# Expert layers whose rows move block by block through per-expert DRAM regions, in place of a sort, a gather and a scatter in each layer

## The chip, the cores and the metric

The kernel runs on one core of a Trainium2 chip. The metric is the device time of one execution in microseconds (us), as the median of several runs. Within the core work TensorE (PE: matrix products and transposes), VectorE (DVE), ScalarE (ACT) and GpSimd (POOL); SyncE (SP) and POOL issue the transfers between DRAM and the on-chip memory. Each engine takes its instructions in the order of the program and waits at semaphores for the others.

## The reference

2,048 tokens (32 sequences of 64) of 128 numbers go through three stages, each added to the running value x after a layer norm: a cross attention with 16 heads over 128 context rows, a linear recurrence over time, and four routed expert layers that share the weights of 16 experts (W1 is 128 x 512 and W2 512 x 128 for each, in float32). All of this document happens in the last stage:

```
def _unipool_layer(xt, router, W1, W2):       # xt is 2048 x 128, router 128 x 16
    probs = softmax(xt @ router);  w = max(probs);  idx = argmax(probs)
    for each expert i:  acc += where(idx == i, w, 0) * (silu(xt @ W1[i]) @ W2[i])
    return acc
xt = layernorm(x)
for router in routers: xt = _unipool_layer(xt, router, W1, W2)     # 4 layers, no residual between
x = x + xt
```

A layer's input is the output of the layer before it, so the routing of a layer can only begin when outputs of the layer before are there.

## The kernel before

Attention runs over 16 tiles of 128 tokens, the recurrence over all tokens at once; neither is touched but for where x and its normalised copy are held. Then come the four layers, as a loop of two passes over two layers (`layers`). Each layer has two stages.

**Routing** works on all 16 tiles at once. SP loads the 2,048 rows (four transfers, L253), PE transposes them (L696), ACT and DVE copy the transposes out, PE makes the logits (L734) and turns them (L739). A chain of some 40 DVE instructions (L1042 to L1117) takes the softmax, counts for each token how many tokens of its expert stand before it, with the help of products on PE (L750 to L755), and so finds the token's place in an order sorted by expert; two further DVE and POOL steps and 16 products (L763) invert that order. From it come a list `token_i` of the sorted tokens and the tables `piece_expert` and `piece_tile`. PE fills its waits with products that nobody reads (`stay_warm`, L689).

**Pieces.** The sorted rows are 16 tiles; where an expert ends inside a tile the tile is worked on twice, so a layer has up to 31 pieces (`PIECES`), and all 31 are always run. POOL gathers the rows of a tile by an indirect transfer (L382), PE transposes it (L782), ACT copies the transpose out (L525) and copies the W1 of the piece's expert to a fixed buffer (L522); PE makes the hidden units (L793, 4 products, each float32 product in two passes), ACT takes the tanh of half of them (L531), DVE makes silu from that (L1132), PE multiplies with W2 (L806, again 4 products), and DVE adds the result, times the routing weight, to `ysort` (L1142). Each step of the loop `step(i)` holds the turn of tile i, the hidden units of piece i-1 and the output of piece i-2. When a sorted tile is complete, POOL writes its rows back to their tokens' places in DRAM by an indirect transfer (L389). The next layer's load waits for all of these. After the last layer the rows are loaded once more, added to x and stored (L1151, L262).

The lines are printed here as far as the change touches them.

Of the kernel before, what the change touches and what calls it, by code (L numbers as in the profile page):

```python
# [22 lines left out]
def perceiver_block(nc, x, ctx, mask, Wq, bq, Wk, bk, Wv, bv, Wo, bo, A, Wb, bb, Wc, bc, Wd, bd,  # L23
# [15 lines left out]
    PIECES = NT + E - 1  # L39
    PC = 32  # L40
    FC = FF // P
    FIRST = 4
    PAIRS = HEADS // 2
    NV = 5
    assert D == P and T == P and S * 2 == P and NG == 4 and E == 16 and L % 2 == 0

    x_t = x.rearrange("b s d -> (b s) d").rearrange("(t p) d -> p t d", p=P)
    out_t = out.rearrange("b s d -> (b s) d").rearrange("(t p) d -> p t d", p=P)
    ctx_t = ctx.rearrange("b t d -> t b d")
    rows = [nc.dram_tensor(f"token_rows_{i}", (N, D), F32, kind="Internal").ap() for i in range(2)]  # L50
# [4 lines left out]
    with ExitStack() as stack:  # L55
# [3 lines left out]
        def sem(name):  # L59
# [11 lines left out]
        rnow = sb("rnow", [P, 32])  # L71
# [17 lines left out]
        iota_r = sb("iota_r", [P, P])  # L89
        iota_j = sb("iota_j", [P, PC])  # L90
        iota_e1 = sb("iota_e1", [1, E])
        sorted_pos = sb("sorted_pos", [P, NT])
        not_first = sb("not_first", [P, GW])
        not_first16 = sb("not_first16", [P, 256])
        vals = sb("vals", [P, NT, NV], BF16)

        xs = sb("xs", [P, NT, D])
        cur = sb("cur", [P, NT, D])
# [24 lines left out]
        lgT = sb("lgT", [P, 512])  # L123
        ex, eq, nth, rk = (sb(n, [P, 256]) for n in ("ex", "eq", "nth", "rk"))
        ohb = sb("ohb", [P, 256], BF16)
        mx, sm, wt, ends, starts, place, wr = (sb(n, [P, 16]) for n in
                                               ("mx", "sm", "wt", "ends", "starts", "place", "wr"))
        place_i, row_i, tile_i = (sb(n, [P, NT], I32) for n in ("place_i", "row_i", "tile_i"))
        ohr = sb("ohr", [P, NT, P], BF16)
        oht = sb("oht", [P, NT, NT], BF16)  # L130
        carried = sb("carried", [P, NT, NV, NT], BF16)
        token_i = sb("token_i", [P, NT], I32)
        token, expert_at, piece_at, wsort = (sb(n, [P, NT]) for n in ("token", "expert_at", "piece_at", "wsort"))
        ends_cmp = sb("ends_cmp", [P, NT, E])
        piece_hot = sb("piece_hot", [P, PC, NT])
        wpiece = sb("wpiece", [P, PC])
        end_i = sb("end_i", [1, E], I32)
        first_piece = sb("first_piece", [1, E])
        pcmp = sb("pcmp", [1, PC, E - 1])
        pexp, pexp_tile = sb("pexp", [1, PC]), sb("pexp_tile", [1, PC])  # L140
        piece_expert = sb("piece_expert", [1, PC], I32)
        piece_tile = sb("piece_tile", [1, PC], I32)


        xin = ppT[:, 2, :].rearrange("p (u d) -> p u d", u=4)
        xT = vm[:].rearrange("p u n x -> p (u n x)")[:, 0:N]
        ysort = sb("ysort", [P, NT, D])
        th, hh, w1_piece = pp[:, 0:2, :], pp[:, 2:4, :], ppT[:, 0:2, :]

        names = """x_first_loaded x_loaded w_loaded later_loaded w1_loaded w2_loaded stored rows_stored  # L150
            consts_pool consts_dve consts_mm dve_step act_step
# [4 lines left out]
            router_ready logits_done lgT_ready lg_done sh_ready ex_ready oh_ready rank_mm  # L156
            tiles_hot carried_ready inv_in inv_done tokens_ready pieces_ready y_zeroed
            nmax_ready xo_ready rden_ready rstd_ready
            waited_alone xT_mm xT_evac w1_staged h_mm tanh_done h_ready y_mm y_ready
            out_ready""".split()  # L160
        s = dict(zip(names, [sem(n) for n in names]))
        ctx_loaded = [sem(f"ctx_loaded{u}") for u in range(2)]
# [30 lines left out]
        def piece_steps(step):  # L193


            for i in range(PIECES + 2):
                step(i)
# [980 lines left out]
```

## Time and profile before

| what | value |
|---|---|
| median of 3 runs | 573.17 us (569.8, 573.17, 573.19) |
| span of the profiled execution | 577.5 us, 4.3 us over the median |
| up to the first transpose of layer 1 | 188.3 us |
| routing of layer 1, up to the first transpose of a gathered tile | 24.8 us |
| pieces of the four layers | 63.96, 63.86, 64.02, 65.84 us |
| between the layers | 30.22, 32.87, 30.50 us |
| after the last product | 13.17 us |
| busy over the span | PE 85%, PE weight loads 69%, DVE 57%, ACT 48%, POOL 34% |

The profiled execution has no device time of its own beside its span, so the span stands for it. A stage is best read by its own borders: the first transpose of a gathered tile (L782) opens the pieces of a layer, the last output product (L806) closes them. PE's busy share in the routing stages is mostly `stay_warm`, so it says nothing on what bounds those.

### The profile page before, as it was taken

What the parts mean: (1) busy time and instruction counts of PE and PEld (TensorE: products, weight loads), DVE (VectorE), ACT (ScalarE), POOL (GpSimd) and SP (SyncE); (2) the same over time, 40 slices, a digit from 0 to 9 for tenths busy, and PEclk for the clock granted to TensorE, in tenths of its full rate; (3) what the DMA queues carried; (4) which work ended last, traced back from release to release, by engine and by line L of the source; (5) the groups of instructions that cost most, each with busy time, mean ns of one, the idle gap of its engine ahead of it and who ended that gap; (6) DMA issues with size and microseconds to landing.
All of it is one profiled execution on the core that took longest, in us unless ns stands there. A gap on an engine that the chain in (4) does not pass through costs nothing.

```text
span 577.5 us, 16903 instructions
## 1 busy us (share of the span) xinstructions
PE 490.8 (85%) x5788; PEld 400.5 (69%) x5788; DVE 330.0 (57%) x746; ACT 276.8 (48%) x684; POOL 196.7 (34%) x243
## 2 busy tenths in 40 slices
PE   1589999999787769999868999976899986799894
PEld 1367877787554338999435999733899953589892
DVE  2468777877658684455185455339345526645452
ACT  1277766777672316665103666410566610266550
POOL 8222332231030154235325405503532541541352
PEclk9999999999999889999997999978899999799998
DMA  5542223300000201001301100120110130100005
GB/s 142 178 130 85 66 86 94 93 5 4 3 1 2 73 18 35 24 20 40 91 1 37 33 8 37 41 74 5 42 31 10 39 100 3 32 28 16 24 37 159
DMA packets 37315, 28.12 MB, mean 49 GB/s; under 512 B 5105, under 2 KB 33137, under 8 KB 37233
## 3 DMA queue, kind: packets, MB, share of 16 engines
q1 hardware_dynamic: 33136, 18.62, 11.2%
q0 software_dynamic: 4096, 8.40, 4.6%
q8 instruction: 52, 0.85, 0.6%
q14 instruction: 31, 0.25, 0.1%
HBM read 20.71 MB, written 6.29 MB: 47 GB/s over the span
## 4 chain that ended last, share of the span: by engine, by line
PE 59%; DVE 15%; issue 7%; DMA 6%; ACT 5%; POOL 3%; another core or an unknown queue 2%; SPq 1%; DVEq 0%; POOLq 0%; ACTq 0%
PE bank L806 18%; PE bank L793 18%; PE bank L635 6%; PE bank L616 4%; DMA cur<-token_rows 3%; PE bank L594 3%; DVE ohr L1083 2%; DVE ppT L910 2%; DMA ppT<-token_rows,token_i 2%; DMA token_rows<-ysort,token_i 2%; PE bank L588 1%; PE bank L575 1%; PE bank L564 1%; PE bank L782 1%
## 5 line engine op out<-in xcount | busy, mean ns | idle before, releaser
L1132 DVE SCALAR_TENSOR_TENSOR pp<-pp,bank 128x512 f32<-128x512 f32 x124 | 85.3, 688 | 126.8 <-ACT pp L531 116.0
L806 PE MATMUL bank<-w,pp 128*128 x992 | 136.3, 281 | 9.0 <-DVE pp L1132 6.9
L793 PE MATMUL bank<-vm,ppT 128*128 x992 | 137.4, 283 | 0.0
L806 PEld LDWEIGHTS bank<-w,pp 128*128 128x128 f32 x992 | 122.5, 194 | 11.7 <-issue 10.9
L793 PEld LDWEIGHTS bank<-vm,ppT 128*128 128x128 f32 x992 | 125.1, 198 | 1.6 <-issue 0.5
L531 ACT ACTIVATE pp<-bank 128x512 f32<-128x512 f32 x124 | 74.1, 598 | 95.6 <-PE bank L793 77.8
L522 ACT COPY ppT<-w 128x512 f32 x124 | 75.8, 611 | 60.2 <-DVE piece_tile L1105 59.7
L389 POOL DMA_INDIRECT token_rows<-ysort,token_i x64 | 62.1, 971 | 102.9 <-DVE ysort L1142 85.2
L382 POOL DMA_INDIRECT ppT<-token_rows,token_i x64 | 61.7, 964 | 64.2 <-PE bank L782 41.3
L689 PE MATMUL bank<-trib,onesb 128*128 128x512 bf16 x308 | 77.4, 409 | 0.0
L446 ACT ACTIVATE pp<-bank,nmax 128x128 f32<-128x128 f32 x256 | 68.0, 426 | 0.0
L689 PEld LDWEIGHTS bank<-trib,onesb 128*128 128x128 bf16 x308 | 31.6, 105 | 37.3 <-issue 9.3
L318 POOL TENSOR_TENSOR qm<-qT,own_head 128x256 f32<-128x256 f32 x32 | 19.0, 614 | 85.0 <-ACT kT L436 85.0
L895 DVE TENSOR_REDUCE nmax<-bank 128x4 f32<-128x512 f32 x64 | 41.0, 684 | 11.4 <-PE bank L594 11.4
L1142 DVE SCALAR_TENSOR_TENSOR ysort<-bank,wpiece,ysort 128x128 f32 x124 | 42.9, 346 | 7.5 <-PE bank L806 6.1
L616 PE MATMUL bank<-ident,pp 128*128 128x128 f32 x256 | 40.8, 282 | 7.3 <-DVE ppT L910 5.7
L616 PEld LDWEIGHTS bank<-ident,pp 128*128 128x128 f32 x256 | 27.4, 141 | 14.7 <-ACT pp L446 10.1
L454 ACT COPY ppT<-bank 128x512 f32<-128x512 f32 x32 | 18.9, 590 | 32.8 <-PE bank L616 32.8
L373 POOL TENSOR_TENSOR carried<-oht,vals 128x256 bf16<-128x256 bf16 x12 | 12.4, 1057 | 56.4 <-DVE oht L1074 56.4
L910 DVE COPY ppT<-bank 128x512 f32<-128x512 f32 x32 | 20.7, 686 | 9.1 <-PE bank L635 8.8
L782 PE MATMUL bank<-ident,ppT 128*128 128x128 f32 x64 | 18.3, 285 | 6.3 <-DMA ppT<-token_rows,token_i 6.3
L594 PEld LDWEIGHTS bank<-kT,qm 32*128 32x128 f32 x512 | 16.5, 194 | 7.2 <-issue 7.2
(182 smaller groups left out, 522.8 us busy)
## 6 DMA issues: line engine op xcount, KB each, us to landing
w<-in_L_ffn_W_dram SPq DMA_DIRECT2D x32, 256.0 KB, 3.4
cur<-token_rows SPq DMA_DIRECT2D x16, 256.0 KB, 3.6
cx<-in_ctx_dram SPq DMA_DIRECT2D x16, 128.0 KB, 2.4
token_rows<-cur SPq DMA_DIRECT2D x1, 1024.0 KB, 5.0
ppT<-token_rows,token_i POOLq DMA_INDIRECT x64
token_rows<-ysort,token_i POOLq DMA_INDIRECT x64
out_dram<-xs SPq DMA_DIRECT2D x4, 256.0 KB, 2.7
xs<-in_x_dram SPq DMA_DIRECT2D x1, 768.0 KB, 6.1
```

The source lines that it names most:

```text
L382: g.indirect_dma_start(out=xin[:, i % 4, :], out_offset=None, in_=src, in_offset=bass.IndirectOffsetOnAxis(ap=token_i[:, i:i + 1], axis=0)) \
L389: g.indirect_dma_start(out=dst, out_offset=bass.IndirectOffsetOnAxis(ap=token_i[:, i:i + 1], axis=0), in_=ysort[:, i, :], in_offset=None). ...
L446: last = a.activation(pp[:, r, k * T:(k + 1) * T], banks[r][:, k * T:(k + 1) * T], ACT.Exp, bias=nmax[:, r, k:k + 1], scale=1.0)
L522: a.copy(w1_piece[:, i % 2, :], w1[:, ds(e * FF, FF)]).then_inc(s["w1_staged"], 1)
L531: a.activation(th[:, j % 2, :], banks[2 + j % 2][:, :], ACT.Tanh, scale=0.5) \
L616: last = nc.tensor.transpose(bank[:, k * P:(k + 1) * P], pp[:, r, k * P:(k + 1) * P], ident[:])
L689: mm(bank[:, :].rearrange("p (k t) -> p k t", k=4), onesb[:], trib[:].unsqueeze(1).broadcast_to([P, 4, P]), start=True, stop=True)
L793: last = mm(banks[2 + j % 2][:, c * P:(c + 1) * P], w1_piece[:, j % 2, c * P:(c + 1) * P], xT[:, ds(tile_of[j] * P, P)], start=True, stop= ...
L806: last = mm(banks[6 + j % 2][:, 0:D], hh[:, j % 2, c * P:(c + 1) * P], w2[:, ds(e * FF + c * P, P)], start=(c == 0), stop=(c == FC - 1))
L895: v.tensor_reduce(out=nmax[:, r, :], in_=banks[r][:, :].rearrange("p (k t) -> p k t", k=4), axis=AX, op=ALU.max, negate=True).then_inc(s[" ...
L1132: v.scalar_tensor_tensor(hh[:, j % 2, :], th[:, j % 2, :], 1.0, banks[2 + j % 2][:, :], ALU.add, ALU.mult).then_inc(s["h_ready"], 1)
L1142: v.scalar_tensor_tensor(sorted_tile, banks[6 + j % 2][:, 0:D], wpiece[:, j:j + 1], sorted_tile, ALU.mult, ALU.add).then_inc(s["y_ready"], 1)
```

## The change

The sort, the gather and the second indirect transfer go. A token's row travels as 274 numbers (1,096 bytes): its value, its 16 logits for the coming layer, a stamp, its token number, and x (`ROW`). There are two DRAM buffers with a region of 2,176 rows for each expert and one spare. In each layer up to 31 blocks of 128 rows are loaded from the regions by plain transfers (`load_rows`, SP, one for each block, at a row number read from `block_row`), computed, and the new rows are scattered by expert into the other buffer (`scatter_part`, POOL). The logits of the next layer are made block by block: PE turns each block's output (`turn_output`) and multiplies it with the next router (`next_logits`). DVE picks the expert of a part of 1 to 4 blocks (`choose`), PE ranks (`ranks`), DVE gives places (`put`), POOL scatters the part. After the last part DVE makes the tables of the next layer (`make_tables`). The routing weight is worked out beside the blocks, for four groups of blocks (`gate_shift`, `gate_finish`), from the logits in the loaded rows. ACT takes silu in one instruction. The last layer adds x and scatters straight to the output, 31 indirect transfers. The loop over layers is written out. The rows for the pads of all regions are written once, during attention, by two SP transfers of 128 x 17 x 274 numbers. W1 stays on chip in both versions and ACT copies it block by block into one of two buffers.

```diff
-            def one_layer(layer, parity, two):      # POOL: 16 gathers, then 16 scatters
-                for i in range(NT):                 # L382
-                    g.indirect_dma_start(out=xin[:, i % 4, :], out_offset=None, in_=src, ...)
-                for i in range(NT):                 # L389
-                    wait_alone(pool, s["y_ready"], layer * PIECES + (i + E))
-                    g.indirect_dma_start(out=dst, ..., in_=ysort[:, i, :], in_offset=None)
+            def scatter_part(number, of_part, region):                          # POOL
+                wait_alone(pool, s["place_ready"], number + 1)
+                for j in of_part:
+                    g.indirect_dma_start(
+                        out=region, out_offset=bass.IndirectOffsetOnAxis(ap=place_i[:, j:j + 1], axis=0),
+                        in_=slots[:, j, :], in_offset=None, bounds_check=E * REGION - 1, oob_is_err=False) \
+                        .then_inc(s["scattered"], 16)
-            def load_next(layer, source): ...       # SP: four loads of 256 KB, L253
+            for layer in range(L):                                              # SP
+                sp.wait_ge(s["scattered"], 16 * (NT + layer * BLOCKS))
+                sp.wait_ge(s["tables_ready"], 2 * layer + 2)
+                for j in range(BLOCKS):
+                    load_rows(layer, j)
+        parts = [list(range(a, min(a + 4, 24))) for a in range(0, 24, 4)] + [[24, 25, 26], [27, 28, 29], [30]]
+        gate_groups = [(0, 4), (4, 10), (10, 20), (20, BLOCKS)]
+        gate_steps = [0, 4, 9, 16]
+                for i in range(BLOCKS + 4):                                     # ACT
+                    if i < BLOCKS:
+                        stage_w1(layer, i)
+                    if 0 <= i - 1 < BLOCKS:
+                        silu(layer, i - 1)
+                    if 0 <= i - 3 < BLOCKS and layer < L - 1:
+                        evac_yT(layer, i - 3)
+                    if i in gate_steps:
+                        gate_half_tanh(layer, gate_steps.index(i))
+            stay_warm(banks[7], 50)                                             # PE, ahead of layer 1
+            def turn_output(layer, j):
+                pe.wait_ge(s["y_evac"], n + 1)
+                nc.tensor.transpose(banks[4][:, 0:P], tile_n(j), ident[:]).then_inc(s["yT_mm"], 1)
+            def next_logits(layer, j):
+                pe.wait_ge(s["yT_evac"], n + 1)
+                mm(banks[7][:, 0:E], yTs[:, n % 2, :], rt[:, layer + 1, :], start=True, stop=True)
+                for i in range(BLOCKS + 4):                                     # PE
+                    ... turn(i), hidden(i - 1), turn_output(i - 3), next_logits(i - 4), output(i - 2)
+                        for m, of_part in enumerate(parts):
+                            if of_part[-1] == (i - 4 if i == BLOCKS + 3 and m == len(parts) - 1 else i - 5):
+                                ranks(part_number(layer, m), len(of_part))
+                if layer < L - 1:
+                    stay_warm(banks[7], 30)
+            def gate_shift(layer, k):                                           # DVE
+                lo, hi = gate_groups[k]
+                for j in range(lo, hi):
+                    dve.wait_ge(loaded[j], 16 * (layer + 1))
+                for i in range(BLOCKS + 6):                                     # DVE
+                    ... evac_xT(i), gate_shift at 0, 4, 9, 16, gate_finish one step later,
+                    ... evac_logits(i - 4), evac_y(i - 2), put of the part that ends at i - 5,
+                    ... choose of the part that ends at i - 4
+                if layer < L - 1:
+                    make_tables()
```

PE, one step of the block loop in a layer (`pp` holds the hidden units, `ppT` and `slots` the rows, `w_piece` the copied W1). Before, for a step with a gathered tile:

```order
L782 MATMUL bank<-ident,ppT 128x128
L793 ISA
L793 MATMUL bank<-vm,ppT 128x128 x2
L200 TENSOR_LOAD piece_tile
L793 MATMUL bank<-vm,ppT 128x128 x2
L200 TENSOR_LOAD piece_expert
L806 ISA
L806 MATMUL bank<-w,pp 128x128
```

The L806 pair stands four times there. With the change, a step after which a part of four blocks is ranked:

```order
L202 TENSOR_LOAD block_expert
L775 MATMUL bank<-ident,slots 128x128
L784 MATMUL bank<-xTs,w_piece 128x128 x4
L803 MATMUL bank<-ident,slots 128x128
L810 MATMUL bank<-rt,yTs 128x16
L794 ISA
L794 MATMUL bank<-w,pp 128x128
...
L753 MATMUL bank<-ohb,onesb 128x64
L757 MATMUL bank<-ohb,trib 128x48
L753 MATMUL bank<-ohb,onesb 128x48
L753 MATMUL bank<-ohb,onesb 128x32
L753 MATMUL bank<-ohb,onesb 128x16
L758 MATMUL bank<-ohb,trib 128x16
```

All 31 blocks now have a turn, and a second one, a product of 16 columns and a share of the ranking are new; the 8 large products are the same.

DVE, the end of a layer with the change, from the places of the part of blocks 27 to 29 on (before, some 40 rows of routing stood between two layers):

```order
L1054 TENSOR_TENSOR rk<-bank,next_at 128x48
L1056 TENSOR_TENSOR rk<-rk,ohb 128x48
L1057 TENSOR_REDUCE place<-rk 128x3
L1061 TENSOR_TENSOR place_i<-outside,place 128x3
L1063 TENSOR_TENSOR next_at<-next_at,bank 128x16
L1044 TENSOR_REDUCE mx<-slots 128x1
...
L1061 TENSOR_TENSOR place_i<-outside,place 128x1
L1063 TENSOR_TENSOR next_at<-next_at,bank 128x16
L1070 TENSOR_TENSOR blocks_i<-next_at,round_up 128x16
...
L1078 TENSOR_SCALAR block_row<-first_row,lane_rows 128x1
L1080 TENSOR_SCALAR block_expert<-expert 128x1
```

The last two rows end `make_tables`, on which SP's first load and ACT's and PE's first block wait.

SP between two layers. Before:

```order
L207 ISA
L207 REGISTER_ALU
L253 DMA cur<-token_rows 128x4x128 x4
L257 REGISTER_ALU
L257 COMPARE_AND_BRANCH
```

With the change, the pads' two transfers and the first loads (with what they wait for):

```order
L244 DMA expert_rows<-slots 128x17x274 x2
L202 TENSOR_LOAD block_row [waits tables_ready,scattered,pads_written]
L250 ISA
L250 DMA slots<-expert_rows 128x274
L202 TENSOR_LOAD block_row
```

Four loads became 31, each with a table entry read into a register ahead of it.

## Rows read from the trace of the kernel before

**Rows 1.** Busy time by stage; columns: stretch, length, busy us (count) of PE, PEld, DVE, ACT, POOL, clock, DMA.

```profile
188.26:213.06 24.80, 17.01 (x98) 8.49 (x99) 18.71 (x51) 5.50 (x11) 7.21 (x7) 0.86 0.16 45
213.06:277.02 63.96, 61.07 (x513) 59.91 (x514) 30.94 (x64) 37.23 (x77) 27.00 (x29) 0.97 0.10 32
277.02:307.24 30.22, 21.96 (x127) 10.13 (x125) 17.97 (x48) 2.21 (x4) 8.79 (x8) 0.94 0.14 42
307.24:371.10 63.86, 61.10 (x513) 59.85 (x514) 30.82 (x64) 37.28 (x77) 27.05 (x29) 0.97 0.10 32
371.10:403.97 32.87, 24.34 (x127) 11.04 (x124) 18.07 (x48) 3.49 (x5) 8.87 (x9) 0.84 0.13 40
403.97:467.99 64.02, 61.17 (x513) 59.95 (x514) 30.93 (x64) 37.25 (x77) 26.96 (x29) 0.97 0.10 32
467.99:498.49 30.50, 21.98 (x127) 10.14 (x125) 18.04 (x48) 2.21 (x4) 8.85 (x9) 0.94 0.14 42
498.49:564.33 65.84, 61.73 (x513) 60.03 (x514) 31.08 (x64) 37.27 (x77) 26.98 (x29) 0.97 0.10 30
564.33:577.50 13.17, 6.04 (x29) 2.55 (x26) 3.12 (x5) 0.00 (x0) 3.50 (x3) 0.83 0.59 169
```

**Rows 2.** Timeline, weight loads; columns: start, duration, instruction, count: pieces without turns.

```profile
247.99 0.97 PEld L793 LDWEIGHTS bank<-vm,ppT 128*128 128x128 f32 x8
260.50 0.97 PEld L793 LDWEIGHTS bank<-vm,ppT 128*128 128x128 f32 x8
```

**Rows 3.** Timeline, weight loads of the turns: twelve pieces with a turn, first and last.

```profile
222.57 0.14 PEld L782 LDWEIGHTS bank<-ident,ppT 128*128 128x128 f32 x1
244.24 0.14 PEld L782 LDWEIGHTS bank<-ident,ppT 128*128 128x128 f32 x1
```

**Rows 4.** Timeline, PE: the ranking products in layer 2.

```profile
293.96 1.01 PEld L750 LDWEIGHTS bank<-ohb,onesb 128*128 128x128 bf16 x15
```

**Rows 5.** Timeline: between layers 1 and 2 (an idle time and its releaser stand in brackets).

```profile
275.87 1.15 PE L806 MATMUL bank<-w,pp 128*128 x8 [0.60 <-DVE pp L1132]
277.18 0.35 DVE L1142 SCALAR_TENSOR_TENSOR ysort<-bank,wpiece,ysort 128x128 f32 x1 [1.19 <-PE bank L806]
278.32 0.97 POOL L389 DMA_INDIRECT token_rows<-ysort,token_i  x1 [0.57 <-issue]
280.64 2.01 SPq L253 DMA_DIRECT2D cur<-token_rows  x4
...
303.46 0.17 DVE L1093 TENSOR_TENSOR token_i<-bank,token 128x16 int32<-128x16 f32 x1
304.45 1.23 POOL L382 DMA_INDIRECT ppT<-token_rows,token_i  x1 [3.10 <-DVE token_i L1093]
305.99 0.96 POOL L382 DMA_INDIRECT ppT<-token_rows,token_i  x1 [0.30 <-issue]
307.24 0.33 PE L782 MATMUL bank<-ident,ppT 128*128 128x128 f32 x1 [0.53 <-DMA ppT<-token_rows,token_i]
307.61 0.27 ACT L525 COPY vm<-bank 128x128 f32<-128x128 f32 x1 [0.52 <-PE bank L782]
```

**Rows 6.** Timeline, DVE: two chained instructions of 16 and of 256 numbers.

```profile
295.58 0.17 DVE L1066 TENSOR_TENSOR starts<-ends,bank 128x16 f32<-128x16 f32 x1
295.78 0.42 DVE L1068 TENSOR_TENSOR rk<-bank,starts 128x256 f32<-128x256 f32 x1
```

**Rows 7.** Timeline: ACT's second activation of layer 2, with its idle time.

```profile
314.47 0.60 ACT L531 ACTIVATE pp<-bank 128x512 f32<-128x512 f32 x1 [3.13 <-remote]
```

**Rows 8.** Timeline, DVE: the last transposes copied out in layer 1.

```profile
191.15 0.69 DVE L1032 COPY curT<-bank 128x512 f32<-128x512 f32 x1 [0.85 <-PE bank L696]
```

**Rows 9.** The page's DMA issues: line, engine, count, KB each, median us to landing.

```profile
cx<-in_ctx_dram SPq DMA_DIRECT2D x16, 128.0 KB, 2.4
token_rows<-cur SPq DMA_DIRECT2D x1, 1024.0 KB, 5.0
```

**Rows 10.** Chain of waits: a table entry read into a register (start, us, queue, line).

```profile
275.62 0.30 DVEq L200
```

More of the change, by code:

```diff
@@ new lines, in perceiver_block @@
+        eq, nth, rk, away = (sb(n, [P, 4 * E]) for n in ("eq", "nth", "rk", "away"))
+        ohb = sb("ohb", [P, 2, 4 * E], BF16)
+        place = sb("place", [P, 4])
+        place_i = sb("place_i", [P, BLOCKS], I32)
+        token_i = sb("token_i", [P, BLOCKS], I32)
+        next_at = sb("next_at", [P, E])
+        blocks_i = sb("blocks_i", [P, E], I32)
+        blocks = sb("blocks", [P, E], I32)
+        ends, past, row_at = (sb(n, [P, E]) for n in ("ends", "past", "row_at"))
+        expert, first_row = sb("expert", [P, 1]), sb("first_row", [P, 1])
@@ L536, in _, with stage_w1 @@
-            layers(act, one_layer)
+            for q in (0, 2):
+                act.wait_ge(s["t_done"], 4 + q + 1)
+                a.copy(curT[:, q * 512:(q + 1) * 512], banks[q][:, :]).then_inc(s["t_evac"], 1)
+            a.preload_act_table(ACT.Silu)
+            def stage_w1(layer, j):
+                n = layer * BLOCKS + j
+                e = entry(block_expert, j, mybir.EngineType.Activation, E - 1)
+                if n >= 2:
+                    act.wait_ge(s["h_mm"], n - 1)
+                a.copy(w1_piece[:, n % 2, :], w1[:, ds(e * FF, FF)]).then_inc(s["w1_staged"], 1)
@@ new lines, in silu, with evac_yT @@
+            def silu(layer, j):
+                n = layer * BLOCKS + j
+                act.wait_ge(s["h_mm"], n + 1)
+                if n >= 2:
+                    act.wait_ge(s["y_mm"], n - 1)
+                a.activation(hh[:, n % 2, :], banks[2 + n % 2][:, :], ACT.Silu).then_inc(s["h_ready"], 1)
+            def evac_yT(layer, j):
+                n = layer * BLOCKS + j
+                act.wait_ge(s["yT_mm"], n + 1)
+                if n >= 2:
+                    act.wait_ge(s["lg_mm"], n - 1)
+                a.copy(yTs[:, n % 2, :], banks[4][:, 0:P]).then_inc(s["yT_evac"], 1)
@@ new lines, in _, with turn @@
+            first_logits(0)
+            first_logits(1)
+            ranks(0, 4)
+            first_logits(2)
+            ranks(1, 4)
+            first_logits(3)
+            ranks(2, 4)
+            ranks(3, 4)
+            stay_warm(banks[7], 50)
+            def turn(layer, j):
+                n = layer * BLOCKS + j
+                pe.wait_ge(loaded[j], 16 * (layer + 1))
+                if n >= 2:
+                    pe.wait_ge(s["xT_evac"], n - 1)
+                nc.tensor.transpose(banks[n % 2][:, 0:P], tile_n(j), ident[:]).then_inc(s["xT_mm"], 1)
@@ new lines, in hidden @@
+            def hidden(layer, j):
+                n = layer * BLOCKS + j
+                pe.wait_ge(s["xT_evac"], n + 1)
+                pe.wait_ge(s["w1_staged"], n + 1)
+                if n >= 2:
+                    pe.wait_ge(s["h_ready"], n - 1)
+                for c in range(FC):
+                    last = mm(banks[2 + n % 2][:, c * P:(c + 1) * P], w1_piece[:, n % 2, c * P:(c + 1) * P],
+                              xTs[:, n % 2, :], start=True, stop=True)
+                last.then_inc(s["h_mm"], 1)
```

599 lines of the change are left out of this document (267 added, 332 removed).

## The prediction

> **What bounds the kernel now.** I read the busy time by stage first, because the change leaves everything up to 188 us alone but for where rows are held. The four stretches of pieces take 63.96, 63.86, 64.02 and 65.84 us, with weight loads busy for 60 of 64 us: there PE is the bound. The three stretches between them take 30.22, 32.87 and 30.50 us, together 93.6; PE's products there are filler, and DVE (18 us of 30) and transfers set the pace. The first routing takes 24.8, the end 13.17 [rows 1]. Then the timeline: a piece without a turn repeats every 1.79 us (247.99 to 260.50, seven periods), so one of its 16 passes costs 0.11 [rows 2]; with a turn it is 1.97 (222.57 to 244.24, eleven periods) [rows 3]. Fifteen pieces of 1.79 and sixteen of 1.97 make 58.4; what is left of 63.95, 5.6 us, is the filling of the pipeline. 3.1 of it is one idle time of ACT with a releaser the profile doesn't know [rows 7].
>
> So the change trades: PE gets more to do in each block, where it is the bound, and most of the routing leaves the path between layers.
>
> **The change part by part.** The sum is made against the span of 577.5 us, which is 4.3 over the median; the difference is carried over to the median.
>
> *Up to 188 us: nothing.* POOL's constants change by a few small fills, either way. The pads are two writes of 2.38 MB, issued behind the last weights, when the transfers are nearly idle. At the rate of the 1 MB store (5.0 us) [rows 9] they take some 24 us, and the first scatter is 80 us away. Were that cover gone, SP's first load would wait 24 us.
>
> *Block.* The 8 large products stay: 1.79. Each block has a turn at 0.18, as now [rows 2, 3]; the second turn is one pass between two others, 0.11; the logits two passes whose 16 columns hide no weight load, 0.22; six ranking products for four blocks at 1.01/15 [rows 4], 0.10. That is 2.40. Below, with both turns packed at 0.11, 2.33; above, both at 0.18, 2.47. ACT has the same copy and activation, and a copy of 0.27 [rows 5]: 1.4 of 2.40, covered. DVE has two copies of 0.35, a small one of 0.17, and nine chained instructions of 64 numbers for four blocks. The price of those: 16 numbers take 0.17 and 256 take 0.42, the next starts 0.03 later [rows 6], so 64 take 0.22, with the hop 0.25. With the gates some 1.8 us of 2.40: covered on the mean. The tight place is the second turn: DVE starts on an output 0.16 after the product's end and takes 0.35 [rows 5], while PE has a turn and four hidden products (1.0) ahead of it.
>
> *Filling.* DVE's own silu step (0.69) goes, but DVE now stands at block 0's gates until four rows' loads have landed, and behind it wait the copy of block 1's transpose and ACT's tanh. Loads are spaced by a register read of 0.30 [rows 10] and an issue of 2.01/4 = 0.50 [rows 5], so three more take 2.4. Part of that runs beside ACT's idle time. I take 5.6 - 0.7 + 1.6 = 6.5; bounds 3.4 (no idle time of 3.1) and 8.
>
> *Layers 1 to 3.* 31 x 2.40 + 6.5 = 80.9 for 63.95: 3 x 17.0 = **+50.9**.
>
> *Between layers*, counted from the end of the last output product. Output copied by 0.51; turned by 0.9 (0.33); copied by ACT by 1.2; logits of block 30 by 1.65. Meanwhile the logits of block 29 are copied (1.3), and the part 27 to 29 is chosen, four instructions, by 2.4; ranked by 3.0; its places are there after four more, at 3.95. POOL's first scatter follows its token list by 0.82 (303.63 to 304.45), the next come 1.26 apart [rows 5]. The three of this part and, after a wait of 0.28, that of block 30 bring the last scatter's start to 8.85; block 30's places (6.3) and the tables (8.4) are earlier. From the last scatter's start to SP's load is 2.32 (278.32 to 280.64) [rows 5], the register read 0.30, the landing of 128 KB 2.4 [rows 9]: 13.9. For 93.6 in three now 41.7: **-51.9**. The filler of 30 products ends before that.
>
> *First layer.* The last transposes are copied out at 191.84 [rows 8]; ACT's table load now follows its copies. Logits of the first quarter 0.9 and 0.16, copies and choosing of two quarters 1.3 each, places 1.0: 196.5. POOL starts at 197.3 and issues 16 scatters: 15 x 1.26 and three waits of 0.28 make 217.0 for the last. Then 2.32, 0.30 and 2.4: 222.1 for the first turn, which is at 213.06 now: **+9.0**. All scatters must land ahead of any load; before, tiles came one by one while PE worked. For the filler of 50 products nobody waits.
>
> *Layer 4* has no second turn and no logits: 31 x 1.97 + 6.5 = 67.6 for 65.84: **+1.8**. *End:* last output copied 0.51, POOL 0.82, landing 2.32: 3.65 for 13.17, **-9.5**.
>
> Sum: 50.9 - 51.9 + 9.0 + 1.8 - 9.5 = +0.3. From the median 573.17 that gives **573.5**. What is late next in a layer is again PE.
>
> **A rule weighed.** The 31 loads are spaced 0.80 by SP, and the 1 MB store moves 140 KB in 0.7 [rows 9], so I let SP set the pace. The Trainium skill speaks against the change here: "DMA: Bandwidth & Descriptors", Bandwidth, Measured, gives 0.95 us for 64 KB and 6.15 for 1 MB and calls small transfers descriptor-dominated. Between its two figures 140 KB would take 1.35 us, an estimate, and the sum would be some 22 us more by the count of rival B. The trace has no load of 140 KB.
>
> **The rivals.**
>
> A, *faster: the idle time of filling doesn't come back.* ACT's 3.13 us [rows 7] stand about the third piece of each layer, with no named cause; nothing says that a program without loop has them. Against: two of the four layers don't follow a jump back and have them too. 4 x 3.1 less: 561.
>
> B, *slower: the loads come late.* DVE asks for blocks 4 to 9 at step 4, some 8.2 us after the first turn (filling, then 2.4 a step); at 0.80 the ninth lands at 7.2. It decides from a spacing of 0.91. At half as much again, 1.2, it lands at 10.8: 2.6 late in four layers, 584. For it: register read and address stand in SP's queue ahead of each load; 0.30 is DVE's price, not SP's. Against: the 1 MB store's rate.
>
> C, *slower: POOL's price goes with bytes.* Its 0.97 us are for rows of 512 bytes; at 1,096 they would be 2.08. Exposed are 16 scatters ahead of layer 1 and 4 in each of three gaps: 28 x 1.11 = 31, 604. It decides from 0.2 more for each. Against: gather and scatter of the same 128 rows take 0.96 and 0.97 though one reads and one writes DRAM [rows 5], which fits a price by rows. The same page (SWDGE vs HWDGE vs iDMA) has a GpSimd core compute one pair of descriptors for each operation, by which C falls; no run here shows a longer row.
>
> D, *slower: DVE's order holds PE.* 1.8 us of work in 2.40, in order, with waits for rank products, gates and loads between the copies that PE needs. The gates' six instructions of up to 176 numbers (0.35 each) stand ahead of an output's copy, which then comes 0.3 late. It decides from 0.06 for each block; at 0.15, 93 x 0.15 = 14, 587.
>
> **The numbers.** Forecast 0.33, alone 564 to 582 (block 2.33 to 2.47: 6.5 either way; filling +6). A 0.28, B 0.14, C 0.12, D 0.13. About 1%, 5.7 us, is what a measurement of this kernel tells from no change: 567.4 to 578.9. Of the forecast 0.05 lies below and 0.06 above, of A 0.25 below; of B 0.12, of C 0.11 and of D 0.11 above. So faster 0.30, slower 0.40, within 0.30. The range is 555 (A with the packed block, 561 - 6.5) to 598 (B and D together, 10 + 14, or C at four fifths); it leaves out the rest of C and what lies beyond these mixtures, less than 0.2.
>
> **What would show it.** First turn of layer 1 at 222 (at 240, C). Period of the turns 2.40 in layers 1 to 3 and 1.97 in layer 4; over 2.5 with PE idle on a DVE copy is D. From a layer's last output product to the next layer's first turn 14 us, with POOL's last four scatters 1.26 apart. Idle time of DVE on loads at step 4 is B; no idle of 3 us in ACT's first three activations is A. The prediction is wrong if the block isn't PE's to bound, or if between layers something other than POOL's queue comes last.

## The result, and the profile after

The changed kernel takes **580.15 us** (median of 5 runs, 577.12 to 582.67) against 573.17 (median of 5): 1.0155 times as long, 95% interval 1.0100 to 1.0209. A second comparison gave 578.93 against 570.06, 1.0156 [1.0112, 1.0201]. So the change makes the kernel 1.6% **slower**. In the runs of the changed kernel the time is 1.8 us above the span of the same execution.

The first view to read is the busy time by stage of the changed kernel's profiled execution (span 575.3); it answers to [rows 1] and has their columns: stretch, its length, busy us (count) of PE, PE's weight loads, DVE, ACT, POOL, then granted clock, DMA share, GB/s. The stages are: up to the last transposes, first routing, then a layer and a gap (the stretch from a layer's last output product to the next layer's first turn) in turn, and the end.

```profile
0.00:193.59 193.59, 160.10 (x3237) 122.75 (x3237) 131.26 (x295) 114.37 (x353) 50.66 (x100) 0.97 0.32 91
193.59:227.63 34.04, 21.28 (x123) 12.51 (x122) 12.09 (x57) 4.89 (x10) 15.79 (x16) 0.81 0.21 72
227.63:306.60 78.97, 74.56 (x656) 72.91 (x656) 43.44 (x185) 40.49 (x95) 23.41 (x24) 0.95 0.29 83
306.60:320.59 13.99, 10.58 (x44) 4.62 (x44) 5.50 (x32) 0.88 (x2) 6.81 (x7) 0.76 0.11 25
320.59:398.61 78.02, 73.31 (x657) 71.83 (x655) 43.49 (x185) 40.63 (x95) 23.42 (x25) 0.98 0.28 82
398.61:411.53 12.92, 9.13 (x43) 4.11 (x43) 5.50 (x32) 0.88 (x2) 6.79 (x7) 0.87 0.08 16
411.53:490.94 79.41, 73.41 (x656) 72.01 (x656) 43.50 (x185) 40.72 (x95) 23.41 (x24) 0.98 0.29 83
490.94:504.92 13.98, 10.57 (x44) 4.61 (x43) 5.50 (x32) 0.88 (x2) 6.81 (x7) 0.76 0.13 29
504.92:570.22 65.30, 60.78 (x528) 59.25 (x526) 27.53 (x97) 34.64 (x65) 28.68 (x30) 1.00 0.29 79
570.22:575.29 5.07, 0.00 (x0) 0.00 (x0) 0.35 (x1) 0.00 (x0) 1.41 (x2) 0.79 0.01 0
```

The trade is there as forecast: the gaps fall from 30 to 34 us to 13 or 14, the layers grow to 78 or 79. But 575.3 lies *below* the 577.5 of the kernel before, while the medians say the opposite. So the two executions that happened to be profiled can't be subtracted, and the kernel before was profiled once more (first experiment).

Next the block loop. The rows are weight loads of two turns eight blocks apart in layer 2 and two nine blocks apart in layer 4, in the timeline of the changed kernel: 18.23/8 = **2.28** a block with second turn, logits and ranks (products that rank the tokens of a part), 17.08/9 = **1.90** without.

```profile
371.43 0.14 PEld L775 LDWEIGHTS bank<-ident,slots 128*128 128x128 f32 x1
389.66 0.14 PEld L775 LDWEIGHTS bank<-ident,slots 128*128 128x128 f32 x1
...
545.49 0.14 PEld L775 LDWEIGHTS bank<-ident,slots 128*128 128x128 f32 x1
562.57 0.14 PEld L775 LDWEIGHTS bank<-ident,slots 128*128 128x128 f32 x1
```

That makes 31 x 2.28 = 70.7 of the 78 or 79 us of a layer. In the same timeline two blocks of each of layers 1 to 3 take far longer: 3.3 us pass between the turns of blocks 11 and 12 (counted from 0), 4.4 to 4.7 between those of 18 and 19. (In layer 4 two blocks take 3.1 and 3.3 for 1.90.) The rows around the period of 4.7, in layer 2, show DVE, and PE with the idle time in brackets:

```profile
360.22 0.29 DVE L1101 COPY xTs<-bank 128x128 f32<-128x128 f32 x1
360.43 0.24 DVE L1118 TENSOR_SCALAR gr<-gd 128x176 f32<-128x176 f32 x1
360.70 1.25 DVE L1119 RECIPROCAL gr<-gr 128x176 f32<-128x176 f32 x1
361.99 0.34 DVE L1120 SCALAR_TENSOR_TENSOR gr<-gd,gr 128x176 f32<-128x176 f32 x1
...
363.48 0.35 DVE L1137 TENSOR_SCALAR slots<-bank,gate 128x128 f32<-128x128 f32 x1
363.88 0.33 PE L803 MATMUL bank<-ident,slots 128*128 128x128 f32 x1 [1.96 <-DVE slots L1137]
```

An output's copy (363.48) stands behind six instructions of the gates in DVE's order. One of them is a reciprocal of 176 numbers, 1.25 us; PE is idle for 1.96. And that isn't all it costs, as the granted clock shows (windows of the same execution, last columns): it falls to 0.50, the 1.2 GHz level, right behind PE's idle time. That does not always follow: in layers 1 and 3 the same idle time (1.91 and 1.96) leaves the clock at 1.00.

```profile
360.00:364.90 4.90, 2.94 (x26) 2.75 (x26) 3.92 (x13) 2.40 (x7) 3.00 (x4) 1.00 0.13 40
364.90:368.30 3.40, 3.40 (x19) 3.40 (x18) 0.72 (x3) 1.06 (x4) 0.89 (x1) 0.50 0.18 67
...
```

The gap between layers 1 and 2 answers to [rows 5]. POOL's last four scatters start 1.27 to 1.28 apart, the last one 8.26 after the last output product; SP's first load is issued 2.57 behind it, the first turn comes 3.16 later. The L686 row is PE's filler, and the last row is the first turn of layer 3.

```profile
305.45 1.15 PE L794 MATMUL bank<-w,pp 128*128 x8
311.03 0.97 POOL L364 DMA_INDIRECT expert_rows<-slots,place_i  x1 [0.76 <-issue]
...
311.20 9.55 PE L686 MATMUL bank<-trib,onesb 128*128 128x512 bf16 x30
...
314.86 0.97 POOL L364 DMA_INDIRECT expert_rows<-slots,place_i  x1 [0.30 <-issue]
...
317.43 26.07 SPq L250 DMA_DIRECT2D slots<-expert_rows  x31
320.59 0.38 PE L775 MATMUL bank<-ident,slots 128*128 128x128 f32 x2
...
411.53 0.33 PE L775 MATMUL bank<-ident,slots 128*128 128x128 f32 x1 [0.38 <-DMA slots<-expert_rows]
```

So this gap ends with the filler (311.20 + 9.55 = 320.75, an end that the profile models) and not with the load: the clock is 0.50 from 311.2 to 317.0, and the 30 products take 9.55. The gap behind layer 3 ends in the same way (filler of 9.54). In the one behind layer 2 the filler takes 7.93, PE then waits 0.38 for the load, 2.10 pass from the load's issue to the first turn, and the gap is 12.92.

A scatter of rows of 1,096 bytes takes 0.97, as the one of 512 bytes did [rows 5], and 31 loads are issued in 26.07, 0.84 each. The page's DMA issues answer to [rows 9] (count, KB each, median us to landing):

```profile
slots<-expert_rows SPq DMA_DIRECT2D x124, 137.0 KB, 2.3
```

### The profile page after: what moved, and what is told of

It is laid out like the page before. It is cut to its first block, busy times and chain, and to the rows that moved or that the text cites. A ratio compares the mean times of both kernels' runs of the same rounds, so it can differ in the third digit from the quotient of the medians.

```text
span 575.3 us, 17287 instructions
## 1 busy us (share of the span) xinstructions
PE 493.7 (86%) x5979; PEld 424.6 (74%) x5979; DVE 318.2 (55%) x1100; ACT 278.4 (48%) x718; POOL 187.2 (33%) x240
## 4 chain that ended last, share of the span: by engine, by line
PE 64%; DVE 17%; issue 8%; POOL 4%; ACT 3%; DMA 2%; SPq 1%; DVEq 0%; POOLq 0%; ACTq 0%
PE bank L794 18%; PE bank L784 16%; PE bank L632 6%; PE bank L613 5%; PE bank L591 3%; POOL expert_rows L364 2%; PE bank L803 2%; PE bank L775 2%; DVE ppT L931 2%; DVE gr L1119 2%; PE bank L810 2%; PE bank L585 1%; PE bank L561 1%; PE bank L572 1%; DMA slots<-expert_rows 1%
## 5 line engine op out<-in xcount | busy, mean ns | idle before, releaser
L364 POOL DMA_INDIRECT expert_rows<-slots,place_i x109 | 106.4, 976 | 219.4 <-DVE place_i L1061 159.9
L784 PE MATMUL bank<-xTs,w_piece 128*128 128x128 f32 x992 | 135.5, 281 | 6.2 <-DVE xTs L1101 5.3
L784 PEld LDWEIGHTS bank<-xTs,w_piece 128*128 128x128 f32 x992 | 124.4, 197 | 7.7 <-DVE xTs L1101 7.6
L500 ACT COPY w_piece<-w 128x512 f32 x124 | 77.2, 622 | 35.8 <-DVE block_expert L1080 33.3
L1137 DVE TENSOR_SCALAR slots<-bank,gate 128x128 f32<-128x128 f32 x93 | 32.7, 351 | 68.4 <-PE bank L794 67.8
L1101 DVE COPY xTs<-bank 128x128 f32<-128x128 f32 x124 | 35.2, 284 | 38.4 <-issue 19.3
L686 PE MATMUL bank<-trib,onesb 128*128 128x512 bf16 x192 | 51.9, 437 | 0.0
L378 POOL DMA_INDIRECT out_dram<-slots,token_i x31 | 30.1, 971 | 42.2 <-DVE slots L1140 38.1
L775 PE MATMUL bank<-ident,slots 128*128 128x128 f32 x124 | 35.1, 286 | 9.1 <-DMA slots<-expert_rows 9.1
L686 PEld LDWEIGHTS bank<-trib,onesb 128*128 128x128 bf16 x192 | 20.8, 110 | 28.1 <-issue 12.3
L803 PE MATMUL bank<-ident,slots 128*128 128x128 f32 x93 | 26.3, 283 | 10.9 <-DVE slots L1137 10.9
L515 ACT COPY yTs<-bank 128x128 f32<-128x128 f32 x93 | 24.2, 261 | 15.9 <-PE bank L803 15.9
```

The costliest lines, as they stand in the source:

```text
L364: g.indirect_dma_start(out=region, out_offset=bass.IndirectOffsetOnAxis(ap=place_i[:, j:j + 1], axis=0), in_=slots[:, j, :], in_offset=Non ...
L500: a.copy(w1_piece[:, n % 2, :], w1[:, ds(e * FF, FF)]).then_inc(s["w1_staged"], 1)
L686: mm(bank[:, :].rearrange("p (k t) -> p k t", k=4), onesb[:], trib[:].unsqueeze(1).broadcast_to([P, 4, P]), start=True, stop=True)
L775: nc.tensor.transpose(banks[n % 2][:, 0:P], tile_n(j), ident[:]).then_inc(s["xT_mm"], 1)
L784: last = mm(banks[2 + n % 2][:, c * P:(c + 1) * P], w1_piece[:, n % 2, c * P:(c + 1) * P], xTs[:, n % 2, :], start=True, stop=True)
L803: nc.tensor.transpose(banks[4][:, 0:P], tile_n(j), ident[:]).then_inc(s["yT_mm"], 1)
```

## The experiments

Each edit is made to the changed kernel (or, where said, to the one named), and the ratio is against the kernel before on the same chip.

**The kernel before, once more.** No edit.

> The kernel before, unchanged, for the spread of its executions. The execution profiled first had a span of 577.5 us, some 6 over what its median of 573.17 stands for (in the runs of the changed kernel the time is 1.8 above the span). Theory 1: that execution was slow by chance, so the spans lie about 571 and a new trace shows which stretch was longer in the first one. Theory 2: a profiled execution is always longer than the timed ones; then the spans lie about 577 again while the times stay at 573.

570.67 us, 0.9995 [0.9964, 1.0025]; the new profiled execution has a span of 569.4. Theory 1 holds. Its layers, in the view and columns of [rows 1], and below them ACT's second activation of layer 2 in the timeline, which answers to [rows 7]:

```profile
214.55:276.71 62.16, 60.60 (x513) 59.75 (x514) 30.93 (x64) 37.26 (x77) 26.97 (x29) 0.97 0.10 33
307.07:369.15 62.08, 60.56 (x513) 59.59 (x514) 30.75 (x64) 37.38 (x78) 27.04 (x29) 0.97 0.10 32
403.20:464.44 61.24, 59.27 (x513) 58.23 (x514) 30.91 (x64) 37.19 (x77) 26.97 (x29) 1.00 0.10 33
494.56:556.51 61.95, 60.49 (x513) 59.75 (x514) 30.74 (x64) 37.25 (x77) 27.05 (x29) 0.97 0.10 32
```

```profile
312.27 0.60 ACT L531 ACTIVATE pp<-bank 128x512 f32<-128x512 f32 x1 [0.28 <-PE bank L793]
```

The layers are 1.8, 1.8, 2.8 and 3.9 us shorter than in the first execution, 10.3 together, more than the whole difference of 8.1 between the spans. The idle time of 3.13 with an unknown releaser isn't there: ACT waits 0.28 for PE. What it was stays open; it belonged to that execution, not to the kernel.

**The changed kernel, once more.** No edit.

> The changed kernel, unchanged, beside the others on one chip: ratio 1.010 to 1.021 if the first comparison holds. Theory of the pads: the part up to the last transposes ahead of the routing (PE's first product of line 693) again ends some 5 us later than in the kernel before (193.6 against 188.3), with PE's idle time on the issue of its instructions inside the 16 us of the pads. Rival, chance of the clock: that part is 1 to 5 us long or short in one execution and not in the other, with no place of its own.

578.93 us, 1.0156; profiled span 575.2. The pads' place is confirmed: PE's idle times on issue stand at the same two products as in the first trace (1.49 and 0.76 here, 1.22 and 0.69 there). In neither trace of the kernel before is there one between 105 and 142 us. The last transposes begin at 192.16 here, against 189.82 in the kernel before's second trace: 2.3 late instead of 5, so chance has its part in that figure too.

**Pads in pieces.**

```
-            for region in regions:
-                sp.dma_start(region.rearrange("(e r) c -> r e c", r=REGION)[0:P, :, :], ...)
+                for n in range(3 * (t - 4), min(3 * (t - 3), 2 * (E + 1))) if t >= 4 else []:
+                    sp.dma_start(regions[n // (E + 1)][ds(n % (E + 1) * REGION, P), :], ...)
```

> The two pad writes of 2.38 MB become 34 writes of 140 KB, three in each of 12 attention tiles, beside the loads of weights that are there. Theory, the pads hold up PE's instructions: attention ends 4.4 us sooner than in the changed kernel, and no idle time on issue of over 0.5 us is left between 113 and 140 us; time 4 to 5 us below it. Rival, the slip up to 188 us is the clock's and not the pads': no difference, within 1.5 us. Second rival, the cost goes with the bytes wherever they are written: the slip is spread over twelve tiles and the time stays.

574.53 us, 1.0071 [1.0041, 1.0102]: 4.4 below the changed kernel, as the theory has it; both rivals had the time stay. First the changed kernel: the pads' issue and PE's idle time in the timeline, then two windows with DMA share 0.98 and 1.01, then the queues from 115.5 to 123.0 (queue, packets, MB, share of 16 engines).

```profile
113.81 4.93 SPq L244 DMA_DIRECT2D expert_rows<-slots  x2
125.69 1.62 PE L591 MATMUL bank<-kT,qm 32*128 32x128 f32 x25 [1.22 <-issue]
```

```profile
120.00:125.00 5.00, 4.08 (x90) 2.83 (x90) 3.92 (x8) 3.58 (x13) 0.16 (x1) 1.00 0.98 309
125.00:130.00 5.00, 4.31 (x39) 3.92 (x39) 1.29 (x2) 1.60 (x6) 2.25 (x4) 0.66 1.01 304
```

```profile
q1 hardware_dynamic: 2213, 2.25, 93.7%
q14 instruction: 1, 0.01, 0.3%
```

Now the kernel with the pads in pieces, same windows, same stretch of the queues:

```profile
120.00:125.00 5.00, 4.61 (x116) 3.43 (x115) 3.75 (x9) 3.30 (x12) 0.44 (x1) 1.00 0.01 3
125.00:130.00 5.00, 5.00 (x152) 4.48 (x151) 4.02 (x9) 4.51 (x17) 1.97 (x4) 1.00 0.01 3
```

```profile
...
q8 instruction: 1, 0.02, 0.8%
...
```

While the pads hold all 16 DMA engines, the instruction queue q8 moves nothing in these 7.5 us; with the pads in pieces it does. A fixed stretch can miss a packet by chance (in the second trace of the changed kernel one of q8 lies in it), so the distance between packets, read in windows of 0.5 us, says more: behind q8's packet at 112 to 114 us the next one comes 8.5 to 10 us later in all six traces with the two large writes, and 5 to 6 later in all eight without. In the six, PE's two idle times on issue end 2 to 3 us behind a packet of q8. PE waits for the issue of its instructions, and behind the idle time the clock is half for a while. No idle time on issue is left between 105 and 142 us with the pads in pieces. That q8 carries PE's instructions is read from these coincidences, not shown by itself. The edit cuts the writes and also spreads them over earlier tiles; which of the two counts was not separated.

**Gates behind the output's copy.** The finish of the two larger groups is moved behind `evac_y` and cut in two after the reciprocal.

```
-                    if i - 1 in gate_steps:
-                        gate_finish(layer, gate_steps.index(i - 1))
+                        evac_y(layer, i - 2)
+                    if i - 1 in gate_steps[2:]:
+                        gate_first(layer, gate_steps.index(i - 1))   # up to the reciprocal
+                    if i - 2 in gate_steps[2:]:
+                        gate_rest(layer, gate_steps.index(i - 2))
```

> The gates of blocks 10 to 19 and 20 to 30 (six chained instructions of DVE, among them a reciprocal of 160 or 176 numbers of 1.15 and 1.25 us) are done behind the copy of the output that PE waits for, and in two steps instead of one. Theory, the reciprocals hold PE: the turns' periods of 3.3 at block 10 and 4.4 to 4.7 at block 18 go down to the 2.28 of the others, 1.0 and 2.1 us in each of layers 1 to 3, 1.2 and 1.4 in layer 4, and 1.2 of half clock behind one of them; in all 10 to 13 us below the changed kernel, that is 568 to 571 and no slower than the kernel before. Rival, loads or instruction fetches hold those blocks: the long periods stay where they are, and the time within 2 us.

568.24 us, 0.9968 [0.9933, 1.0004]: 10.7 below the changed kernel, and no slower than the kernel before. In its timeline of layer 2 the period of 4.7 is 2.2, the next one 2.4, and no window from 356 to 368 has a clock under 1.00. The period of 3.3 did not go in layers 1 to 3: it moved one block on (3.30), where the second half of the gates meets the choosing and placing of a part. In layer 4, which has neither, the period of 3.1 fell to 2.26. The layers take 77.50, 74.67, 74.38 and 66.10 in this execution.

**First gates one step later.**

```
-        gate_steps = [0, 4, 9, 16]
+        gate_steps = [1, 4, 9, 16]
```

> The gates of blocks 0 to 3 are asked for at step 1 instead of step 0 of each layer. Theory, a layer's fill is held by DVE and ACT waiting in order for the loads of four rows' gates (ACT's copy of W1 for block 1 stands behind the tanh and begins at 323.07, 2.5 us after the layer's first turn at 320.59; PE waits 1.22 for what hangs on it): 1.0 to 1.4 us less in each of four layers, 4 to 5.5 us below the changed kernel (579). Rival, the loads themselves pace the fill, 0.82 apart: less than 1 us in all.

568.07 us, 0.9967 [0.9938, 0.9995]: 10.5 below the changed kernel (1.0156 of the kernel before, which makes 578.6 on this chip), twice what was expected. The mechanism first, in the changed kernel's timeline at the start of layer 2:

```profile
322.14 0.22 DVE L1108 TENSOR_REDUCE gmax<-slots 128x4 f32<-128x64 f32 x1 [0.90 <-DMA slots<-expert_rows]
322.66 0.26 ACT L520 ACTIVATE gd<-gd 128x64 f32<-128x64 f32 x1 [7.44 <-DVE gd L1109]
323.07 0.62 ACT L500 COPY w_piece<-w 128x512 f32 x1 [0.16 <-issue]
323.79 1.13 PE L784 MATMUL bank<-xTs,w_piece 128*128 128x128 f32 x8 [1.22 <-DVE xTs L1101]
```

DVE stands at the gates until the fourth row has landed, ACT's tanh waits for DVE, W1's copy for block 1 stands behind the tanh, and PE's second block waits for that: it begins 3.20 after the layer's first turn (320.59). With the edit PE begins that block 1.82 after the first turn (317.18):

```profile
317.18 0.59 PE L775 MATMUL bank<-ident,slots 128*128 128x128 f32 x2
...
319.00 1.06 PE L784 MATMUL bank<-xTs,w_piece 128*128 128x128 f32 x8
```

That is 1.4 a layer, the 4 to 5.5 us expected. Where the rest comes from the windows suggest. A layer's fill is its start, until blocks follow each other at their period. In the second trace of the changed kernel the clock is at half in the fills of all four layers; in layer 2:

```profile
319.00:323.00 4.00, 1.76 (x14) 1.55 (x15) 1.93 (x8) 1.39 (x4) 0.00 (x0) 1.00 0.62 175
323.00:326.00 3.00, 3.00 (x17) 3.00 (x16) 0.78 (x5) 1.59 (x3) 0.00 (x0) 0.52 0.63 182
```

To the fifth turn that fill takes 9.66 us; the same fill in the first trace, whose clock fell in the gap ahead of it instead, takes 7.06. So the fill is 2.6 longer where the clock falls in it; the gap ahead is 0.96 shorter (13.03 for 13.99), which leaves 1.6. In the trace with the later gates no fill of layers 2 to 4 has a fall. One trace each shows that this occurs, not how often.

Gap and fill can be taken together, from a layer's last output product to the fifth turn of the next layer. The three stretches sum to 64.9 and 68.1 us in the changed kernel's two traces and to 59.1 with the later gates, and layer 1's own fill to the fifth turn takes 9.7 and 10.1 for 7.9. That is 7.6 to 11.2 less, so the 10.5 lie in what became shorter there.

**More filler ahead of layer 1.** `stay_warm(banks[7], 50)` becomes 78.

> The filler ahead of layer 1 has 78 products instead of 50. Theory, the clock: PE is idle for 7.6 us ahead of the first turn and the granted clock is half from 225 to 235, which makes the first layer's fill 2.6 us longer than a fill at full clock (7.67 against 5.06 to the fourth turn); with the idle time gone 2 to 3 us below the changed kernel. Rival, the fill waits for loads and for DVE, and PE's clock doesn't count there: same time within 1 us. It could also be 1 us slower, if the filler ends later than the first load.

578.63 us, 1.0157 [1.0112, 1.0201]: no difference from the changed kernel's 578.6, as the rival has it. The idle time ahead of the first turn (226.77) is down from 7.66 to 1.16, and yet the clock falls, only later, in the fill itself:

```profile
227.00:231.00 4.00, 1.83 (x11) 1.33 (x10) 1.70 (x7) 0.96 (x3) 0.00 (x0) 0.68 0.61 177
231.00:235.00 4.00, 3.94 (x18) 3.98 (x19) 1.23 (x6) 2.01 (x4) 0.00 (x0) 0.50 0.62 164
```

PE is busy for 1.83 of the 4 us from 227 on. Filler ahead of the fill did not help here, where the fill itself leaves PE idle.

**Last parts in pairs.** `[[24, 25, 26], [27, 28, 29], [30]]` becomes `[[24, 25], [26, 27], [28, 29], [30]]`.

> The last parts of a layer are blocks 24 and 25, 26 and 27, 28 and 29, 30 instead of three, three and one. Theory, POOL's queue of scatters ends the gap: it idles 1.9 us before the scatters of 24 to 26 and 0.76 before those of 27 to 29, then issues 27, 28, 29, 30 one after another; with one scatter less behind the last choice each gap of 13.9 is 1.3 shorter, 3.8 us in all, or 2 to 4 with a fourth choice to pay. Rival, DVE's chain of choices and tables ends the gap: one part more makes each gap 0 to 2 longer.

572.25 us, 1.0043 [1.0011, 1.0075]: 6.4 below the changed kernel, more than expected, and not by the mechanism as expected. The gaps of its trace are 13.80, 12.70 and 14.08, as long as in the changed kernel. The last scatter does start sooner, 7.19 after the last output product (309.25), for 8.26. But the filler ends last (313.98 + 9.23 = 323.21), as in two gaps of the changed kernel's first trace, and the first turn waits for it, 4.05 behind SP's load for 3.16:

```profile
313.98 9.23 PE L686 MATMUL bank<-trib,onesb 128*128 128x512 bf16 x30
...
316.44 0.97 POOL L364 DMA_INDIRECT expert_rows<-slots,place_i  x1 [0.31 <-issue]
...
319.00 6.79 SPq L250 DMA_DIRECT2D slots<-expert_rows  x9
323.05 0.38 PE L775 MATMUL bank<-ident,slots 128*128 128x128 f32 x2
```

By that time more rows have landed, so the gain shows in the fill: 4.18 to the fourth turn of layer 2 for 5.06. Three times 1.07 explains 3.2 of the 6.4. Taken together as above, the three gaps with their fills sum to 60.0, 4.9 and 8.1 below the changed kernel's traces: the 6.4 lie between.

**Five edits together**: pads in pieces, gates behind the copy with steps 1, 4, 8, 16 (8 for 9 takes the third group out of the way of the choosing), 78 fillers, parts in pairs.

> Pads in 34 pieces, gates behind the output's copy in two steps (groups now asked for at steps 1, 4, 8 and 16), 78 fillers ahead of layer 1, and the last parts in pairs. If the five effects add up: 4.4 + 10.7 + 4.5 + 2.5 + 3 below the changed kernel's 579, that is 554, some 16 us (2.8%) faster than the kernel before. If fill, filler and parts bring nothing: 564, 1% faster.

551.22 us, **0.9661 [0.9622, 0.9699]**; the second time, beside the next two kernels:

> The kernel with the five edits once more, on the chip of the next two: 0.962 to 0.970 of the kernel before if the first comparison holds.

552.44 us, 0.9683 [0.9639, 0.9727]. The periods of 3.3 and 4.4 are 2.2 to 2.5, and in the second trace all four layers have the full clock (73.40, 72.39, 72.74 and 62.46 us). The single effects sum to 32.0 (4.4, 10.7, 10.5, 0 and 6.4), the whole is 27.4 (578.6 to 551.2), so some of them overlap.

**Less filler between layers, and pairs to the end** (both on top of the five edits): `stay_warm(banks[7], 30)` becomes 22; then also parts 20 to 22, 23 and 24, 25 and 26, 27 and 28, 29 and 30.

> The five edits, and the filler between layers has 22 products instead of 30. Theory, with the scatters' queue shortened the filler ends the gap: it ends at 311.41, SP loads at 307.55 and a load lands some 2.3 later, so the first turn (311.24) can come 1.3 sooner in each of three gaps: 2 to 4 us below the kernel with the five edits. Rival, the loads of rows 1 to 3, 0.8 apart, pace the fill, so what is gained ahead of it is waited for in it: within 1 us. Second rival, PE then idles ahead of the layer and the clock falls in its fill, which costs 2.6 us where it happens: as slow or slower.

> As the kernel with 22 fillers, and the parts from block 20 on are 20 to 22, 23 and 24, 25 and 26, 27 and 28, 29 and 30: two choices instead of three behind the last output product. Theory, DVE's chain of choices and POOL's queue end together (last places at 303.35, last scatter 304.99): with one choice less the last scatter starts 0.7 to 1.2 sooner, 2 to 3.5 us in all. Rival, the two scatters behind the last choice (1.28 each) take back what the choice gave: within 1 us of the kernel with 22 fillers.

551.04 us, 0.9637 [0.9597, 0.9677], and 551.42, 0.9652 [0.9614, 0.9690]. Neither can be told from the five edits. The gaps with 22 fillers are 12.42, 11.87 and 11.87, for 14.12, 13.53 and 13.08 beside it; but layers 2 to 4 are 0.5, 0.6 and 1.5 longer, because loads come 0.84 apart whenever the first turn does. That is the first rival: 2.6 of the 4.6 gained in the gaps are given back. In layer 4 it is the second as well: the clock falls in its fill (483.5 to 486.9). With pairs to the end the last scatter of layer 1 starts 7.25 after the last output product, for 7.19 with 22 fillers, so its rival holds.

**Without the pairs and the filler.**

> Pads in 34 pieces, gates behind the output's copy in two steps, the first gates one step later; the filler ahead of layer 1 (50) and the last parts (three, three, one) as in the changed kernel. Open is why parts in pairs brought 6.4 us, where the traces show the last scatter 1.07 sooner in each of three gaps. Theory 1, it is the scatters' queue: 3 to 6 us slower than with all five edits (0.966 to 0.968 of the kernel before), that is 0.973 to 0.979. Theory 2, it was the layers' fill, which the late first gates shorten as well, so the two overlap: 0.965 to 0.972.

553.81 us, 0.9694 [0.9665, 0.9723]. It lies in the range of theory 2: with the fills already short, pairs and filler together bring 1 or 2 us instead of 6.4. That speaks for the fill, and so does the trace: the three gaps with their fills sum to 59.6, and to 58.9 with all five edits (second time). By the times alone an effect of the queue of up to 3 us isn't excluded.

## Why the prediction came out as it did

The sum of its steps against both pairs of traces (us; the second pair is the kernel before's second trace, 569.4, and the changed kernel's, 575.2):

| step | forecast | first pair | second pair |
| --- | --- | --- | --- |
| up to the transposes | 0 | +5.3 | +2.3 |
| first routing | +9.0 | +9.2 | +9.1 |
| layers 1 to 3 | +50.9 | +44.6 | +51.7 |
| between layers | -51.9 | -52.7 | -55.6 |
| layer 4 | +1.8 | -0.5 | +6.0 |
| end | -9.5 | -8.1 | -7.8 |
| sum | +0.3 | -2.2 | +5.8 |

**The step that failed is carrying the sum over to the median.** As a span the forecast was 577.5 + 0.3 = 577.8; the five spans first timed have the median 578.3, and that agreement is luck in part, as the terms below show. But 573.5 came from taking off 4.3, on the assumption that what made the profiled execution of the kernel before longer than its median would stay in the changed kernel. (With the 1.8 between span and time, which the kernel before's second trace shows too, that excess was 6.1.) It didn't stay: that was idle time in the fills that the change rewrote. The prediction had these 3.1 us in hand, as rival A: "nothing says that a program without loop has them". True, but neither does the kernel before in its other trace, so no gain could come of it. The sum would have had to start from layers of 62, not 64; that the second pair's +51.7 for layers 1 to 3 is so near +50.9 is luck, because the new layers were forecast some 2 us too long as well. The median lies in the range, and the slower side, the likeliest, is what came; as a mechanism neither B, C nor D alone was it.

**The block:** 2.40 forecast, 2.28 measured, under the lower bound of 2.33; second turn, logits and ranks cost 0.38 together (2.28 - 1.90), not 0.43. Over 93 blocks that is 11 us less. **The gates took them back:** priced at 0.35 for an instruction of 176 numbers, which bounds five of the six; the reciprocal takes 1.25, and the stalls are 1.0 and 2.1 a layer, the second 3.7 where the clock falls behind it. This is D's mechanism, but at two blocks of each layer, not at each; the forecast's 31 equal blocks hid it. The gates' experiment measures the price in time: 10.7. A price was at hand: the kernel before has a reciprocal of 128 numbers, at 0.95, in its own trace (by line and form).

```profile
L916 DVE RECIPROCAL rden<-bank 128x128 f32<-128x128 f32 x16 | 15.2, 948 | 1.8 <-PE bank L635 1.8
```

**The filling** was sized too long: 6.5 forecast; what 31 blocks of 2.28 and the stalls leave of the layers is 5.2, 2.6 and 5.5. The three misses, 11 too dear, 11 too cheap and 6 too dear, make the layers' 44.6 for 50.9 in the first pair.

**The pads** were costed at nothing, with 24 us if their cover went. The cover held, SP's load never waited, and they cost 4.4 all the same; the coincidences above speak for their having taken the DMA engines from PE's instructions. The change part asked who waits for the pads, and not who shares the engines with them.

**First routing** was right to within a microsecond: its last scatter starts at 222.08 and the first turn comes at 227.63, for 217.0 and 222.1 plus the 5.3 by which all starts later. **The gap** is 13.99, 12.92 and 13.98 for 13.9, but ends as described in one of three only. The prediction let the filler end earlier and would call itself wrong if something other than POOL's queue came last; with the clock at half the filler does, by some 1 us. Where it doesn't, the gap is 12.9 to 13.0 (all three of the second trace), so the chain was priced 1 us too dear and the match of the other two is luck. **The end** is 5.07 for 3.65: the last scatter starts at 571.48, and 3.8 pass to the end of the span, for the 2.32 taken.

**C** is out: 0.97 for rows twice as long. **B** is out as a mechanism of its own: at step 4 of layer 2 DVE waits for loads for 0.48, and the turns around it keep their 2.23. The Trainium skill ("DMA: Bandwidth & Descriptors", Bandwidth, Measured) would give some 1.35 us for 137 KB, an estimate between its figures for transfers issued from GpSimd; 31 loads in 26.07 us show 0.84 each, so the rule does not set the pace here.

## What to carry to other kernels

Profile the kernel before twice ahead of subtracting from it: an idle time with no named releaser, the same in each stage of one execution, may belong to the execution. In an engine's in-order queue price the longest instruction by its own kind, and put what nobody waits for soon behind the copy that the next engine waits for; here one reordering was worth 10.7 us. Spread large background transfers in pieces over a longer stretch, even where nobody waits for them: here that gave back 4.4 us.

## What the runs showed of the hardware

- DVE's reciprocal takes 0.55 us for 64 numbers and 1.25 for 176 in each partition, 6.3 ns a number; the addition and product behind it 0.22 and 0.34, 1.1 ns. The Trainium skill ("VectorE: DVE Perf Modes", First, the fixed hardware budget) has it as an iterated division with a repeat count of 8; the trace's ratio is about 6.
- Beside a write of 2 x 2.38 MB that runs at 300 GB/s the packets of the instruction queue q8 come 8.5 to 10 us apart for 5 to 6, and PE stalls on issue between 105 and 142 us (1.22 to 1.49 us at the same product) in all six traces with it, and in none of the eight without it.
- A short idle time of PE can cost twice: once itself, once by the half clock behind it. Behind 1.96 us at layer 2's gates the next block took 3.7 for the 2.2 of layers 1 and 3, where the clock stayed at 1.00; a fall in a fill cost 1.6 more than one in the gap ahead of it.
